# Moving the first-half work of a factorization tower forward by one slice, and fetching one operand through DRAM instead of transposing it

## What is computed

```python
def _cin_layer(X0, Xi, W, b):
    H = W.shape[0]
    Wr = W.reshape(H, F0_, Fi)
    return jnp.einsum('hjk,bjd,bkd->bhd', Wr, X0, Xi) + b[None, :, None]
...
for W, b in Ws:
    Xi = _cin_layer(X0, Xi, W, b)
    res.append(Xi.sum(axis=2))
...
h = jnp.concatenate([z, dense_ctx], axis=1)
h = jnp.maximum(h @ W_top1 + b_top1, 0.0)
h = jnp.maximum(h @ W_top2 + b_top2, 0.0)
y = h @ W_top3
```

## Time and profile before

| | |
|---|---|
| three runs | 1437.16, 1438.17, 1438.38 us, median 1438.17 |
| the profiled execution's own time | 1436.21 us |
| its span | 1434.4 us |
| busy: PE, DVE, ACT, POOL | 1313.6, 1082.4, 1066.5, 892.8 us |
| mean granted TensorE clock | 0.972 of full speed |
| DMA | 87.27 MB in 53451 packets |

### The profile page before, as it was taken

The page is one execution under the profiler, slowest core; times in us unless marked ns, Lnnn a source line. Parts: engine busy times, 40 slices in busy tenths (PEclk is TensorE's granted clock), DMA queues, the critical chain, the costliest instruction groups (busy, mean ns, idle before and its releaser), DMA issues.

```text
span 1434.4 us, 23609 instructions
## 1 busy us (share of the span) xinstructions
PE 1313.6 (92%) x6157; PEld 1061.7 (74%) x6157; DVE 1082.4 (75%) x2678; ACT 1066.5 (74%) x3372; POOL 892.8 (62%) x663
## 2 busy tenths in 40 slices
PE   3179999999999999999999999999999999999986
PEld 3158777777788777887778777887778878887765
DVE  3068989898867987688766988679876988679930
ACT  2238888789867887688867888678876899678942
POOL 6658577868766678666766587667776265341111
PEclk8659999999999999999999999999999999999999
DMA  6242222322221222303231122212232122210010
GB/s 214 51 111 57 51 64 71 84 55 53 72 80 33 65 59 64 76 21 77 62 88 46 44 62 60 80 33 71 53 90 55 29 67 71 78 31 8 9 38 0
DMA packets 53451, 87.27 MB, mean 61 GB/s; under 512 B 15136, under 2 KB 37152, under 8 KB 52032
## 3 DMA queue, kind: packets, MB, share of 16 engines
q1 hardware_dynamic: 43172, 82.64, 21.4%
q0 software_dynamic: 9984, 2.58, 1.9%
q10 hardware_dynamic: 156, 0.48, 0.1%
HBM read 18.47 MB, written 8.39 MB: 19 GB/s over the span
## 4 chain that ended last, share of the span: by engine, by line
PE 54%; POOL 19%; issue 12%; DVE 8%; DMA 3%; ACT 2%; SPq 1%; ACTq 0%; POOLq 0%; DVEq 0%
PE ring L927 12%; PE ring L929 11%; PE ring L928 11%; POOL pairs L396 6%; POOL pairs_lo L407 6%; PE side L825 5%; POOL e_in L364 5%; PE l_ps L812 3%; DVE terms L754 3%; POOL blocks L418 3%; PE side L851 3%; PE l_ps L814 3%; PE l_ps L813 2%; DVE x_s L709 2%; DMA x_rep<-x_t 2%
## 5 line engine op out<-in xcount | busy, mean ns | idle before, releaser
L597 ACT ACTIVATE terms<-ring,e_both 128x128 f32<-128x128 f32 x2944 | 832.2, 399 | 242.9 <-PE ring L929 237.4
L754 DVE SCALAR_TENSOR_TENSOR terms<-ring,e_both,terms 128x128 f32<-128x128 f32 x1792 | 508.4, 344 | 96.7 <-PE ring L929 93.6
L927 PE MATMUL ring<-w_hi,x_hi 128*128 128x512 f32 (+1 forms) x1280 | 546.4, 427 | 32.5 <-DVE terms L754 25.2
L929 PE MATMUL ring<-w_hi,x_lo 128*128 128x512 f32 (+1 forms) x1280 | 500.4, 391 | 0.0
L928 PE MATMUL ring<-w_lo,x_hi 128*128 128x512 f32 (+1 forms) x1280 | 498.8, 390 | 0.0
L709 DVE TENSOR_REDUCE x_s<-terms 128x32 f32<-128x800 f32 x512 | 489.0, 976 | 0.2
L364 POOL DMA_INDIRECT e_in<-in_tbl,idx x312 | 305.8, 980 | 88.6 <-issue 79.0
L407 POOL TENSOR_TENSOR pairs_lo<-pairs,pairs_hi 117x1024 fp32r<-117x1024 f32 (+1 forms) x104 | 250.0, 2404 | 168.0 <-ACT pairs_hi L497 167.0
L927 PEld LDWEIGHTS ring<-w_hi,x_hi 128*128 128x128 f32 x1280 | 242.9, 190 | 106.8 <-DVE terms L754 38.5
L396 POOL TENSOR_TENSOR pairs<-x_rep,pairs 117x1024 f32<-117x1024 f32 (+1 forms) x104 | 250.4, 2408 | 93.2 <-DMA pairs<-x_t 93.2
L928 PEld LDWEIGHTS ring<-w_lo,x_hi 128*128 128x128 f32 x1280 | 243.6, 190 | 49.1
(11 more groups left out here) (64 smaller groups left out, 629.1 us busy)
## 6 DMA issues: line engine op xcount, KB each, us to landing
pairs<-x_t SPq DMA_DIRECT2D x312, 156.0 KB
x_scratch<-x_s SPq DMA_DIRECT2D x32, 256.0 KB, 2.2
x_r<-x_scratch SPq DMA_DIRECT2D x8, 1024.0 KB, 6.0
x_rep<-x_t SPq DMA_DIRECT2D x45, 156.0 KB
g_t<-in_L_rec_W SPq DMA_DIRECT2D x2, 2496.0 KB, 10.3
e_in<-in_tbl,idx POOLq DMA_INDIRECT x312
x_r<-x_t SPq DMA_DIRECT2D x8, 156.0 KB
wtop<-in_W_top SPq DMA_DIRECT2D x1, 768.0 KB
```

The source lines that it names most:

```text
L597: last = nc.scalar.activation(term(d, ACT_BEFORE[d][g] + i), twos(ring[:, (GROUPS * d + g) % RING, i * H:(i + 1) * H]), ACT.Copy, scale=e_ ...
L754: nc.vector.scalar_tensor_tensor(out=acc, in0=y, scalar=e_of[:, j, d:d + 1], in1=acc, op0=ALU.mult, op1=ALU.add).then_inc(dve_unit, 1)
L927: nc.tensor.matmul(acc, x1_hi[:, x], w1_hi[:, w], start=True, stop=False)
L929: nc.tensor.matmul(acc, x1_lo[:, x], w1_hi[:, w], start=False, stop=True).then_inc(y_group, 1)
```

## The change

The change does five things.

1. `xb` no longer comes from PE transposes. SP writes the chunk's embeddings (`e_cur`, now stored column by column) to DRAM after the loads of tile 11 (`x0_write`) and reads them back at the start of the next step in the layout that POOL wants (`xb_back`). The transposes L834, ACT's copies L528 and the waits on them are gone. Samples are in another order inside G because of it, so several copies (g_t, dense, h2, z0) permute columns, and `blocks` is laid out the other way round.
2. The first half's seven tiles are made in slices 7 to 13 instead of 8 to 14 and multiplied in slices 8 to 14. The eighth (the first of the second half) stays in slice 15. The transposes of `x0_t`, the move of the new embeddings, z2, dense, h1, h2 and y are one slice earlier. Layer 0's groups are 4 and 6 instead of 3 and 5.
3. `blocks` has four slots instead of three.
4. The dense product of h1 is padded with zero rows from 16 to 128.
5. z2 takes three products per group instead of two. The table of gathers changes, and SP's loop is written out.

```diff
-    Z2_SLICES, Z2_FROM, Z2_AT_ONCE = (0, 1, 2), 4, 2
-    XB_SLICES, XB_AT = (0, 1), 6
-    DENSE_SLICE = 2
-    H1_SLICE, H1_AT = 3, (6, 7, 8, 9)
-    H2_SLICE = 4
-    Y_SLICE, Y_AT = 5, 7
-    COPY_SLICE, CUR_FROM, MOVE_SLICE = 2, 4, 5
-    X0T_SLICES = (6, 7)
+    Z2_SLICES, Z2_FROM, Z2_AT_ONCE = (0, 1), 4, 3
+    DENSE_SLICE = 1
+    H1_SLICE, H1_AT = 2, (6, 7, 8, 9)
+    H2_SLICE = 3
+    Y_SLICE, Y_AT = 4, 7
+    COPY_SLICE, CUR_FROM, MOVE_SLICE = 1, 3, 4
+    X0T_SLICES = (5, 6)
...
-    L0_AT = [(1, 2) if d == D - 1 else (3, 5) for d in range(D)]
-
-    X1_HI_AT = {1: (6, 7), 0: (15, 4)}
-    X1_LO_AT = {1: (7, 1), 0: (15, 6)}
-    Z0_AT = {1: (7, 7), 0: (15, 8)}
+    L0_AT = (4, 6)
+
+    X1_HI_AT = {1: (6, 7), 0: (14, 7)}
+    X1_LO_AT = {1: (6, 9), 0: (14, 9)}
+    Z0_AT = {1: (7, 7), 0: (15, 7)}
...
-    BLOCK_FIRST, BLOCK_SLOTS = 7, 3
-
-    GATHERS = (3, 3, 3, 3, 3, 0, 6, 5, 1, 1, 2, 2, 1, 2, 1, 3)
-    INDEX_SLICE = 6
+    BLOCK_FIRST, BLOCK_SLOTS = 7, 4
+
+    GATHERS = (3, 3, 3, 3, 0, 4, 7, 1, 1, 1, 1, 1, 1, 1, 6, 3)
+    INDEX_SLICE = 5
...
+                def x0_write():
+
+                    after(sp, e_cur_ready, c + 1)
+                    after(sp, xb_in, 16 * c)
+                    sp.dma_start(x0_dram.rearrange("d b f -> b d f"), e_cur).then_inc(x0_out, 16)
+
+                def xb_back():
+
+                    after(sp, x0_out, 16 * c)
+                    after(sp, block_made, G_GROUPS * (c - 1))
+                    sp.dma_start(xb[:, :, :], x0_dram.rearrange("d (b g) f -> (d b) g f", g=G_GROUPS)
+                                 ).then_inc(xb_in, 16)
...
                     nc.gpsimd.tensor_tensor(
-                        blocks[:, g % BLOCK_SLOTS, :, 0:FIELDS],
-                        xb[1 - odd][:, g:g + 1, :].to_broadcast(shape),
-                        own[:, :].unsqueeze(2).to_broadcast(shape), ALU.mult).then_inc(block_made, 1)
+                        blocks[:, g % BLOCK_SLOTS, 0:FIELDS, :],
+                        xb[:, g, :].unsqueeze(2).to_broadcast(shape),
+                        own[:, :].unsqueeze(1).to_broadcast(shape), ALU.mult).then_inc(block_made, 1)
...
-                            last = nc.tensor.transpose(side[:, 1, i * FIELDS:(i + 1) * FIELDS],
-                                                       x0_t[0:FIELDS, r::G_GROUPS],
-                                                       ident[0:FIELDS, 0:FIELDS])
-                        last.then_inc(xb_ps, 1)
...
-                        for k, z in enumerate((z0[:, odd, :], g_t[:, FIELDS, :], z2_sb, dense_t)):
-                            rows = DENSE if k == 3 else P
+                        for k, z in enumerate((z0[:, odd, :], g_t[:, FIELDS, :], z2_sb, dense_t[:, :])):
```

More of the change, by code:

```diff
@@ L159, in build_tower @@
         x2_r = sb("x2_r", [P, G_GROUPS, H])
-        xb = [sb(f"xb{i}", [P, G_GROUPS, FIELDS]) for i in range(2)]
-        blocks = sb("blocks", [P, BLOCK_SLOTS, SAMPLES_PER_G, GCOLS])
+        xb = sb("xb", [P, G_GROUPS, FIELDS])
+        blocks = sb("blocks", [P, BLOCK_SLOTS, GCOLS, SAMPLES_PER_G])
         g_t = sb("g_t", [P, GCOLS, P])
@@ L230, in build_tower, with by_group, scale_of @@
         block = ctx.enter_context(nc.Block())
+        def by_group(ap):
+            return ap.rearrange("p (g b) -> p b g", b=SAMPLES_PER_G)
+        def scale_of(j, d):
+            return e_mid[:, j, d:d + 1] if d < CUR_FROM else e_cur[:, d, j:j + 1]
         def twos(ap):
@@ L248, in steps @@
             step(1, 1, layer1=True, following=True, previous=True, mlp=False, gathers=True)
-            with eng.Fori(2, CHUNKS - 3, 2) as c:
-                step(c, 0, layer1=True, following=True, previous=True, mlp=True, gathers=True)
-                step(c + 1, 1, layer1=True, following=True, previous=True, mlp=True, gathers=True)
+            if unrolled:
+                for c in range(2, CHUNKS - 2):
+                    step(c, c % 2, layer1=True, following=True, previous=True, mlp=True, gathers=True)
+            else:
+                with eng.Fori(2, CHUNKS - 3, 2) as c:
+                    step(c, 0, layer1=True, following=True, previous=True, mlp=True, gathers=True)
+                    step(c + 1, 1, layer1=True, following=True, previous=True, mlp=True, gathers=True)
             step(CHUNKS - 2, 0, layer1=True, following=True, previous=True, mlp=True, gathers=False)
@@ L334, in step @@
                             x2_back()
+                        if i == X0_AFTER:
+                            x0_write()
                         if following and i in X2_WRITES:
@@ L577, in step @@
                         act.wait_ge(e_cur_ready, c + 1)
-                    e_of = e_mid if d < CUR_FROM else e_cur
                     after(act, x2_done, n - 1)
@@ L632, in _ @@
                                     ALU.add).then_inc(own_made, 1)
+            nc.vector.memset(dense_t[:, :], 0.0).then_inc(dense_cleared, 1)
+            nc.vector.memset(wtop1[:, 3, :], 0.0).then_inc(dense_cleared, 1)
             dve.wait_ge(own_made, 1)
             for i in range(BLOCK_SLOTS):
-                last = nc.vector.tensor_copy(blocks[:, i, :, FIELDS], own[:, :])
+                last = nc.vector.tensor_copy(blocks[:, i, FIELDS, :], own[:, :])
             last.then_inc(own_made, 2)
@@ L901, in side_work @@
                     used = tile_multiplied(c, d, layer1, following)
-                    if used and g in L0_AT[d]:
-                        layer0(*used, L0_AT[d].index(g) * BANK)
+                    if used and g in L0_AT:
+                        layer0(*used, L0_AT.index(g) * BANK)
                 for d in range(D):
```

94 lines of the change are left out of this document (44 added, 50 removed).

## The result

The changed kernel takes 1429.41 us (four runs, 1428.07 to 1430.12) beside 1438.28 for the kernel before (four runs, 1437.16 to 1438.90): 0.9938 of it, 95% interval 0.9921 to 0.9955. It is 9 us faster where 43.7 were forecast, and 15 us outside the range. So times are compared within a set; only sets 3 and 4, whose kernels before lie 0.03 us apart (1438.16 and 1438.19), are compared with each other.

The account below looks back on a forecast made before the run. PE, busy 1313.6 us, was taken to bound most slices, with waits in others. Gains 18 + 12.3 + 19 less 5.8 gave 43.5: 1436.2 profiled to 1392.7, or 1394.5 against the median 1438.2; range 1380 to 1414.

Parts of the forecast that it names:

- One slice earlier: Slices 7 and 8: PE runs 0.83 us further ahead, then waits that much longer; costs 5.8 us over 7 chunks.
- the hole of slice 8: PE's wait for DVE's x1_lo and z0 in slice 8, forecast to grow from 1.71 to 2.5 us.
- DVE takes over at both ends: Rival: DVE's extra 2.5 us show whole in slices 7 and 15, 13 us in all, 1407 us; chance 0.13.
- Transposes 18: PE's side work: two slots of eight transposes at 1.20 us removed in 8 chunks, 19.2, taken as 18 us gained.
- padding 12.3: PE's four h1 slots per chunk fall from 1.29 to 0.905 us each; 12.3 us gained over 8 chunks.
- Rows don't matter: Rival: padding h1's product to 128 rows gains nothing, 12.3 us less won, 1407 us; chance 0.05.
- Circle 19: POOL's circle of G, block, gathers, remainder, layer 0 opens; holes in slices 9, 11, 12, 14, 15 close, 19 us gained.
- one slot's worth, half: Lower bound of the gain from opening POOL's circle: 10 us if only one slot's worth were won.
- Slice 15's hole left at 1.4: x1_lo and z0 lie in slices 14 and 15, where PE is short; the hole there stays at 1.4 us.
- DMAs nothing: SP's x0 write, 8.8 to 14.6 us long, is hidden between tile 11's loads and tile 12's product; costs nothing.
- The rival of a clogged queue: Rival: short writes on SP's queue delay tile 12's load; 1490 us at 0.25 us per packet; chance 0.04.
- z2, blocks, copies nothing: z2 in 13 slots, blocks at 717 ns and ACT's copies with other strides were counted as no change.

Follow-up runs that it names:

- sets 3 and 4: Two groups of follow-up runs of the changed kernel and edited versions; the kernel before took 1438.16 and 1438.19 us in them.
- e1: Changed kernel with the combination of z0 issued in slice 10 instead of slice 7: 1388.64 us, 0.9657 of the kernel before.
- f2: Changed kernel with the combination of z0 left in slice 7, its first input read from PSUM: 1393.96 us, 0.9695 of the kernel before.
- g1: Kernel before with only the operand by DMA and the padding, three block slots: 1446.46 us, 0.9784 of the kernel before.
- f3: e1 with the dense product back on 16 rows, without padding: 1403.65 us, 0.9762 of the kernel before.
- g2: Kernel before with the operand by DMA, the padding and four block slots, nothing moved: 1427.19 us, 0.966 of the kernel before.
- f1: e1 with x0 written behind the loads of tile 13 instead of tile 11: 1383.09 us, 0.961 of the kernel before.

## Why the prediction was wrong, by its own steps

- **The step that failed** is "One slice earlier". It took the durations of all instructions as fixed, counted only the two that DVE gets on top of its ring work there (1.28 and 1.22), and priced the move by PE's wait for them: the hole of slice 8 "grows from 1.71 to 2.5", 5.8 us in all. It left out the third instruction at that place, the combination of 0.35, and asked when POOL's tile 0 would be ready, not what else would run while POOL works on it. In the kernel before POOL's idle 6.67 us were the cover, and the move took them away. Measured in chunk 5, PE's idle time in slices 7 and 8 went from 1.71 us to 6.61, and the low clock behind it cost about 1.7 more (PE busy 11.41 us in slice 8, 9.67 in e1). The missing mechanism costs 38.6 us over all chunks by e1, 33 by f2. What the step did price did not come: with the combination elsewhere (e1) PE is idle 0.27 and 1.14 us in the two slices, 1.41 together, no more than before. PE's own work in slice 7 was 7.34, not 6.88.
- **The rivals.** "DVE takes over at both ends" named the right engine and place, but priced only DVE's own work, at 13 us. No case held a collision of two engines. The page of the Trainium skill that speaks against this change ("SBUF — State Buffer", section "Who interferes with whom") was there, and I did not weigh it.
- **Transposes 18 and padding 12.3**: the two alone (g1) gave 0.9784, 31 us in its set (interval 26 to 37). The padding by itself gave 1.53 us in the h1 slice (forecast 1.54), and 15 us by the medians of few runs, 11.9 between profiled executions. So the rival "Rows don't matter" is out. What the Trainium skill says, page "TensorE: Matmul & The Clock Gate", section "Step-by-step: what each phase is for", is said of the weight load, and there these traces agree (182 ns for 16 rows in f3, 192 for 128 in e1); it is the matmul that is dearer (321 against 275). Why it is, no run shows.
- **Circle 19**: 19.3 us between g1 and g2 by the medians, each known to about 5 us; slices 11, 12, 14 and 15 of chunks 1 to 5 account for 15.1. Size right within that; the bound "one slot's worth, half" was too low, since one edit alone wins all of it.
- **Slice 15's hole left at 1.4**: PE is idle 1.31 in slice 0. Right.
- **DMAs nothing**: the write lands in 7.5 us, near the lower of my two estimates (8.8 and 14.6), and tile 12 never waits for it. But I looked at SP's queue only. Its place costs 5.5 us (e1 against f1) by way of POOL's gathers in chunk 1, so this term was 5.5, not 0. The rival of a clogged queue did not come.
- **z2, blocks, copies nothing**: a block takes 731 ns (717 in the earlier trace rows), ACT's copy of `e_cur` 1325 ns in place of 743, and no wait points at them. Right.
- **The sum**: e1, the change without the collision, takes 1388.6 us, 49.5 less than before in its set, where 43.5 was the sum. Apart from the collision the forecast was 6 us too careful, about the 5.8 that it took off for the half's border and that did not come; that the two agree is partly luck, since the write's 5.5 us were lost, and chunk 0 and the tail gave some 6 us more than the terms had for them. One slip changes nothing: 2.0 added to 1392.7 is 1394.7, not 1394.5.

## What to carry to other kernels

Before a block of work is moved on one engine, list what every other engine executes in the new window, down to instructions of 0.3 us, and for VectorE and GpSimd look at where the operands lie: here an instruction of VectorE with two inputs from SBUF grew from 0.35 us to as much as 5.37 beside GpSimd's work. Keep such instructions in slices where VectorE has slack, or take one input from PSUM. A busy time that rises with an unchanged count of instructions is the sign to look for in the profile, by the least, median and most of each line.
